# A feature-major U by VectorE block transposes in a conditioned residual kernel, with a new order of work at the head

## Chip, cores and metric

The kernel runs on one NeuronCore of a Trainium2 chip. The metric is the device time of one execution in microseconds, taken as the median of several runs. The profile is of one execution of the same program and has its own time.

## The reference, cut to what matters

Two layers are applied to x (2 batches, 2048 rows, 512 features, float32), each added to its input.

```python
U = (mu @ W_dec + b_dec).reshape(B, 513, 30)      # mu: 2 x 256, W_dec: 256 x 15390
weight = U[:, :-1] @ V ; bias = U[:, -1] @ V       # V: 30 x 512
x1 = x + (x @ weight + bias)
...
h = ln(ln(x1, pw_g[path], pw_b[path]), cp_g[c], cp_b[c])
t = ln(x1, tm_g[c], tm_b[c]) ; s = ln(x1, ms_g[k], ms_b[k])
m, n, r = x1 + mlp_ln(memory), x1 + mlp_ln(noise), x1 + mlp_ln(resource)
cat = [w0*h, w1*t, w2*m, w3*n, w4*r, w5*s]         # w = softmax(aw), 3072 features
out = x1 + ln(silu(cat @ int_W1 + b1) @ int_W2 + b2) * g + be
```

The matrix x @ weight is never built. The kernel computes (x @ U) @ V with the rank-30 factor U, so U must lie with the 512 input features on partitions, in 4 chunks of 128, before TensorE can multiply x by it.

## The kernel before, in words

The 4096 rows are worked in 32 tiles of 128 rows, which alternate between the batches. Each engine has one program, ordered by hand, and semaphores tie them together. Names used below:

- `decode(j)`, 16 steps: TensorE multiplies the conditioning vector (cond, 32 columns, 2 of them real) by a piece of W_dec (960 KB) which SyncE has loaded into one of 8 ring slots. Two steps, one per half of the 256 rows, fill one of 8 banks with 32 partitions x 480 columns in each of 4 partition quadrants. `dec_used` counts the steps.
- `evacuate(m)` on ScalarE copies bank m to `Ur`. There U is a row vector on partitions c*32+b (chunk c, batch b). `to_features` moves it by 16 small DMAs (12 issued by GpSimd, 4 by ScalarE) into `Uf`, with features on partitions. VectorE adds b_dec to `Uf` and writes it four times into `Ust` as high and low parts (`ust_ready`).
- `prefill(p)`: the product of a tile's x with the X block of int_W1 for tiles 2 to 13, done between the decode steps so that TensorE has work while W_dec arrives. `pre_high(p)` (ScalarE) and `pre_low(p)` (VectorE) split the operand into two parts, and `pre_keep(p)` (ScalarE) saves the result in the stash. A product is 12 matmuls: high x high, high x low, low x high in 4 chunks.
- `embed(t)`: x @ Ust of a tile; `embedded` (ScalarE) and `stacked` (VectorE) make the operand of `expand(t)`, which multiplies by V. `first_sum` adds x, `x_stats` and GpSimd's `rstd` make the norm, `x_norm` (ScalarE) writes xhat.
- `scaled`, `scale_rows` and `h_first`/`h_gain` make the operands t, s and h. TensorE transposes them (`transpose_t/s/h`), ScalarE and VectorE split them (`t_high`/`t_split` and so on), and `t_product`, `s_product`, `h_product` follow. `silu`, `transpose_z`, `z_split`, `second_product`, `out_stats`, `out_scaled`, `out_row` finish a tile.
- The blocks of int_W1 (`BLK_T`, `BLK_S`, `BLK_H`) and int_W2 (`BLK_W2`), and the small MLPs' weights (`MLP1`, `MLP2[0..2]`) come through the ring after W_dec. `block_high` (ScalarE) and `t_low`, `s_low`, `h_low` (VectorE) split them.
- `mlp_second(m)` and `sum_parts` finish the conditioning vectors, `low_rank_product` and `offset_product` make the small operands VWst and BT.
- All loads but the gathers (`gathers`, GpSimd) are issued by SyncE in one order: the head's order is written out at L437 to L482 and L455 on is the part behind the decode.
- From tile 2 on each engine repeats `step(n)`. Tiles 2 to 13 are the kept ones, whose X product was made ahead by `prefill`.

## Time and profile before

| | |
|---|---|
| median of 3 runs | 614.84 us (613.6 to 614.91) |
| the profiled execution | 613.73 us, span 611.9 us |
| TensorE busy | 584.0 us, 95% |
| VectorE, ScalarE, GpSimd busy | 416.7, 204.7, 389.4 us |
| bytes moved | 102.07 MB |

The span runs from the first to the last instruction; what lies around it in the profiled execution is 1.8 us. A group of instructions is given by its line in the kernel, its engine and the tiles that it writes and reads. The idle time printed with an instruction is what its engine waited just before it.

### The profile page before, as it was taken

The numbers are of one execution on the slowest core, as the hardware profiler recorded it, in microseconds if no ns is written. First come the engines' busy times: TensorE is split into PE (matmuls) and PEld (weight loads), VectorE is DVE, ScalarE is ACT, GpSimd is POOL, SyncE is SP. The second block draws the span as 40 slices with busy tenths as digits, with TensorE's granted clock in tenths as the row PEclk, the third lists the DMA queues.
The fourth block names the chain that finished last, engine by engine and source line by source line (L and its number), as shares of the span: only waits on it lengthen the run. The fifth ranks groups of instructions, "written<-read, shape, count | busy, mean of one in ns | idle before, by whom it ended". The sixth has DMA issues, their size and how long they took to land.

```text
span 611.9 us, 9087 instructions
## 1 busy us (share of the span) xinstructions
PE 584.0 (95%) x2924; PEld 453.9 (74%) x2924; DVE 416.7 (68%) x750; ACT 204.7 (33%) x346; POOL 389.4 (64%) x499
## 2 busy tenths in 40 slices
PE   0999889999999999999999999999999999999995
PEld 0455446588888888888888888888888888888784
DVE  4311277688888888888766676676666666667754
ACT  4333454333334333334233223233322332232222
POOL 1011467568888888888676676666677766666720
PEclk9999999999999999999999999999999999999999
DMA  8999996425544555555433334435443333443201
GB/s 333 406 403 364 351 353 231 148 69 159 160 143 142 162 165 164 147 181 159 144 93 125 125 119 143 123 126 142 142 141 113 130 116 123 120 142 116 79 19 51
DMA packets 51039, 102.07 MB, mean 167 GB/s; under 512 B 9646, under 2 KB 22190, under 8 KB 50876
## 3 DMA queue, kind: packets, MB, share of 16 engines
q1 hardware_dynamic: 38496, 59.54, 28.3%
q0 software_dynamic: 12160, 42.04, 22.4%
q8 instruction: 18, 0.29, 0.2%
q14 instruction: 17, 0.14, 0.1%
q10 hardware_dynamic: 348, 0.06, 0.1%
HBM read 93.11 MB, written 8.39 MB: 166 GB/s over the span
## 4 chain that ended last, share of the span: by engine, by line
PE 83%; DMA 8%; DVE 3%; SPq 2%; issue 2%; POOL 2%; ACT 1%; DVEq 0%; POOLq 0%
PE bank L744 22%; PE bank L745 22%; PE bank L746 22%; PE bank L738 8%; DMA ring<-in_W_dec 5%; DMA ring<-in_int_W 3%; PE bank L795 2%; SPq L333 2%; PE bank L732 2%; PE bank L814 1%; PE bank L810 1%; PE bank L805 1%; DMA pwt<-in_pw,idx 1%; DVE bn L1250 1%; PE bank L886 0%
## 5 line engine op out<-in xcount | busy, mean ns | idle before, releaser
L744 PE MATMUL bank<-W,ops 128*128 128x512 f32 x432 | 177.8, 412 | 0.0
L745 PE MATMUL bank<-W,ops 128*128 128x512 f32 x432 | 171.1, 396 | 0.0
L746 PE MATMUL bank<-W,ops 128*128 128x512 f32 x432 | 170.8, 395 | 0.0
L592 ACT ACTIVATE ops<-bank 128x512 fp32r<-128x512 f32 x97 | 57.1, 590 | 154.0 <-PE bank L738 154.0
L744 PEld LDWEIGHTS bank<-W,ops 128*128 128x128 f32 x432 | 81.7, 189 | 25.2 <-issue 8.4
L746 PEld LDWEIGHTS bank<-W,ops 128*128 128x128 f32 x432 | 81.4, 188 | 19.5
L745 PEld LDWEIGHTS bank<-W,ops 128*128 128x128 f32 x432 | 81.7, 189 | 14.7
L1245 DVE TENSOR_TENSOR ops<-bank,ops 128x512 fp32r<-128x512 f32 x97 | 66.2, 683 | 12.5 <-ACT ops L592 12.5
L1250 DVE BATCH_NORM_STATS2 bn<-h 128x6 f32<-128x512 f32 x32 | 22.2, 693 | 55.2 <-POOL h L1082 55.2
L1022 POOL TENSOR_SCALAR ve<-mv 128x1 f32<-128x1 f32 x94 | 31.3, 333 | 38.7 <-DVE mv L1254 35.3
L641 ACT ACTIVATE xhat<-x,nm,rs 128x512 f32<-128x512 f32 x32 | 26.1, 816 | 82.0 <-POOL nm L1035 82.0
L744 PE MATMUL bank<-W,zop 128*128 128x512 f32 x124 | 49.6, 400 | 0.4 <-DVE zop L1245 0.4
L1082 POOL TENSOR_TENSOR h<-h,pwt 128x512 f32<-128x512 f32 x32 | 47.6, 1489 | 2.5
L745 PE MATMUL bank<-W,zop 128*128 128x512 f32 x124 | 49.0, 395 | 0.0
L746 PE MATMUL bank<-W,zop 128*128 128x512 f32 x124 | 49.0, 395 | 0.0
L1071 POOL TENSOR_TENSOR xop<-stash,xop 128x512 fp32r<-128x512 f32 x18 | 23.2, 1290 | 39.6 <-ACT xop L563 39.6
L1371 DVE SCALAR_TENSOR_TENSOR o<-o,mv,gbc 128x512 f32<-128x512 f32 x31 | 47.7, 1540 | 0.0
L1047 POOL DMA_INDIRECT ctt<-in_ct,idx x32 | 40.4, 1261 | 8.7 <-issue 5.2
L1080 POOL TENSOR_TENSOR h<-xhat,pwt 128x512 f32<-128x512 f32 x32 | 42.8, 1336 | 2.9 <-ACT xhat L641 1.9
L648 ACT ACTIVATE ht<-h,nm,rs 128x512 f32<-128x512 f32 x32 | 26.1, 816 | 54.1 <-POOL nm L1035 54.1
L333 POOL DMA_DIRECT2D Uf<-Ur x12 | 6.5, 565 | 56.6 <-ACT Ur L549 56.6
L1091 POOL TENSOR_TENSOR xb<-x,bebc 128x512 f32<-128x512 f32 x32 | 42.0, 1314 | 0.6
(145 smaller groups left out, 1080.7 us busy)
## 6 DMA issues: line engine op xcount, KB each, us to landing
ring<-in_W_dec SPq DMA_DIRECT2D x16, 960.0 KB, 12.1
x<-in_x SPq DMA_DIRECT2D x32, 256.0 KB
out<-xb SPq DMA_DIRECT2D x31, 256.0 KB
stash<-in_xT SPq DMA_DIRECT2D x30, 256.0 KB, 5.2
ring<-in_int_W SPq DMA_DIRECT2D x4, 1024.0 KB, 9.2
xraw<-in_xT SPq DMA_DIRECT2D x14, 256.0 KB, 2.8
mnr_row<-in_mnr SPq DMA_DIRECT2D x3, 768.0 KB, 7.6
idxrep<-in_rows SPq DMA_DIRECT2D x32, 64.0 KB, 3.8
```

What stands on the lines that cost most here:

```text
L592: nc.scalar.activation(dst.rearrange("p c t -> p (c t)"), bank[:, :], ACT.Copy).then_inc(done, 1)
L738: last = nc.tensor.transpose(dst[:, c * P:(c + 1) * P], src[:, c * P:(c + 1) * P], ident)
L744: nc.tensor.matmul(bank[:, :], op[:, HI, c, :], w[:, HI, c, :], start=start and c == 0, stop=False)
L745: nc.tensor.matmul(bank[:, :], op[:, HI, c, :], w[:, LO, c, :], start=False, stop=False)
L746: last = nc.tensor.matmul(bank[:, :], op[:, LO, c, :], w[:, HI, c, :], start=False, stop=stop and c == KC - 1)
L1022: nc.gpsimd.tensor_scalar(ve[:, which:which + 1], mv[:, which, 1:2], EPS, 1.0, ALU.add, ALU.mult) \
L1047: pool.indirect_dma_start(out=dst[:, s, :], out_offset=None, in_=d[table], in_offset=bass.IndirectOffsetOnAxis(ap=idx[:, s, col:col + 1], ...
L1080: nc.gpsimd.tensor_tensor(h1[:, :], xhat[:, :], pwt[:, s, 0:D], ALU.mult).then_inc(h1_part, 1)
L1082: nc.gpsimd.tensor_tensor(h1[:, :], h1[:, :], pwt[:, s, D:2 * D], ALU.add).then_inc(h1_ready, 1)
L1091: nc.gpsimd.tensor_tensor(xb[:, f.row, :], x1[:, f.slot, :], bebc[:, :], ALU.add).then_inc(xb_ready, 1)
L1245: nc.vector.tensor_tensor(dst.rearrange("p c t -> p (c t)"), bank[:, :], hi.bitcast(F32).rearrange("p c t -> p (c t)"), ALU.subtract).then ...
L1371: nc.vector.scalar_tensor_tensor(out=o[:, :], in0=o[:, :], scalar=mv[:, 2, 0:1], in1=gbc[:, :], op0=ALU.subtract, op1=ALU.mult).then_inc(u ...
```

## The change

U takes another way to the feature partitions. The host orders W_dec so that bank m = 2c+h holds, for chunk c and half h of the ranks, in quadrant g the columns (rank, feature) of 15 ranks x 32 features. One VectorE transpose of each bank in 32x32 blocks (`turn`) puts the feature on the partition. The addition of b_dec then reads `UT` with a stride of 32 elements. `evacuate`, `to_features` and their DMAs are gone. A piece of W_dec is now one run of 7680 bytes per partition, where it had been four of 1920.

The constants are loaded in two parts: what the offsets and selections need (`BL` and what lies behind it, 347.5 of 601.5 KB) comes late (`picks_in`), behind MLP2. The order of loads, and of each engine's head, is new, and so is part of each `step`.

```diff
+            def turn(m):
+                v.wait_ge(dec_used, 2 * (m + 1))
+                nc.vector.transpose(UT[:, m * BANK:(m + 1) * BANK], u_bank_of(m)[:, 0:BANK]).then_inc(u_row, 1)
+            for j in range(2 * DECS):
+                if j % 2 == 1:
+                    turn(j // 2)
+                if j in PRE_AFTER and PRE_AFTER.index(j) + 2 < NPRE - 2:
+                    pre_low(PRE_AFTER.index(j) + 2)
...
-            pre_low(NPRE - 1)
-            v.wait_ge(u_in_pool, 16 * 3 * KC)
-            v.wait_ge(u_in_act, 16 * KC)
+            v.wait_ge(u_row, DECS)
             for b in range(B):
-                last = nc.vector.tensor_tensor(Uf[:, b, :, :], Uf[:, b, :, :], bdec[:, :, :], ALU.add)
+                last = nc.vector.tensor_tensor(
+                    Uf[:, b, :, :], UT.rearrange("p (c r j) -> p j c r", c=KC, j=Q)[:, b, :, :], bdec[:, :, :], ALU.add)
...
+            pre_low(NPRE - 2)
+            pre_low(NPRE - 1)
```

Loads (SyncE):

```diff
-                    load(sp, cst_in, (cst[:, :], d["cst"]))
+                    load(sp, cst_in, (cst[:, 0:AT_BL], d["cst"][:, 0:AT_BL]))
...
             load_ring(sp, MLP1)
+            load_pre(NPRE - 2)
+            load_x(Tile(1))
             load_rows(Tile(0))
-            load_pre(NPRE - 2)
-            load_pre(NPRE - 1)
+            load_rows(Tile(1))
             load_ring(sp, BLK_T)
+            load_pre(NPRE - 1)
             load_ring(sp, MLP2[0])
-            load_x(Tile(1))
             load_ring(sp, MLP2[1])
             load_ring(sp, MLP2[2])
+            load(sp, picks_in, (cst[:, AT_BL:CST], d["cst"][:, AT_BL:CST]))
             load_ring(sp, BLK_S)
-            load_rows(Tile(1))
             load_ring(sp, BLK_H)
-            load_rows(Tile(2))
+            load_x(Tile(2))
             load_ring(sp, BLK_W2)
-            load_x(Tile(2))
+            load_rows(Tile(2))
```

Heads of ScalarE (first part) and TensorE (second part), as lines taken out and put in:

```diff
             embedded(t0)
+            x_high(t1)
             block_high(T_, WT, BLK_T, t_block_hi)
-            x_high(t1)
             x_norm(t0)
+            embedded(t1)
             t_high(t0)
-            embedded(t1)
+            evict_part((mlp_used, 4), mlp_part)
+            block_high(S_, WS, BLK_S, s_block_hi)
             pre_keep(NPRE - 1)
-            block_high(S_, WS, BLK_S, s_block_hi)
-            evict_part((mlp_used, 4), mlp_part)
+            x_high(t2)
+            h_norm(t0)
             s_high(t0)
...
+            embed(t0)
+            prefill(NPRE - 1, FRONT)
             pe.wait_ge(silu_ready, 1)
             transpose_rows(HIDT, hid, hidT_sum)
-            embed(t0)
-            prefill(NPRE - 1, FRONT)
+            expand(t0)
+            x_half(t0, 0)
             prefill(NPRE - 1, BACK)
-            expand(t0)
             mlp_second(0)
             embed(t1)
             mlp_second(1)
-            x_half(t0, 0)
+            mlp_second(2)
             transpose_t(t0)
-            mlp_second(2)
+            transpose_s(t0)
             x_half(t0, 1)
             sum_parts(sel_m, mlp_part, mlp_sum, start=False)
-            transpose_s(t0)
+            expand(t1)
             x_half(t1, 0)
-            expand(t1)
```

In GpSimd's head `x_low(t0)` comes before `gathers(t0)`, `x_low(t1)` behind `rstd(0, t0)`, and `gathers(t1)` behind `rstd(1, t0)`. In VectorE's head both `one_hot` come first and `scale_rows` ahead of `scaled` for tile 0. Behind the offset product TensorE does `s_product(t1)` before `transpose_h(t1)` and `sum_parts(sel_bt, ...)`.

In every step: TensorE does `transpose_h(m)` behind `t_product(m)`, where it came before; ScalarE does `h_high(m)` before `z_high(c)`; VectorE does `scaled` before `scale_rows`, `h_split` before `out_scaled`, and `one_hot` ahead of `s_split`.

## Rows read from the trace of the kernel before

**Rows 1.** The page's busy time: engine, us, share of span, instructions

```profile
PE 584.0 (95%) x2924; PEld 453.9 (74%) x2924; DVE 416.7 (68%) x750; ACT 204.7 (33%) x346; POOL 389.4 (64%) x499
```

**Rows 2.** Waits of TensorE over the span: total us, times, longest

```profile
PE bank L732 <- DMA ring<-in_W_dec: 17.2, 3, 15.6
PE bank L874 <- ACT part L596: 1.7, 2, 0.9
PE bank L795 <- DVE Ust L1240: 1.2, 1, 1.2
PE bank L795 <- POOL xop L1071: 0.8, 1, 0.8
...
PE bank L738 <- DVE tt L1289: 0.2, 1, 0.2
```

**Rows 3.** Windows: length, PE, PEld, DVE, ACT, POOL busy; clock, DMA share, GB/s

```profile
2.00:15.40 13.40, 0.00 (x0) 0.00 (x0) 7.59 (x14) 6.21 (x10) 0.51 (x3) 1.00 0.99 379
...
61.50:77.00 15.50, 14.25 (x59) 7.65 (x60) 4.05 (x14) 6.37 (x9) 6.59 (x8) 1.00 1.01 358
...
200.00:300.00 100.00, 100.00 (x504) 82.66 (x504) 87.60 (x158) 37.80 (x65) 85.14 (x107) 1.00 0.52 158
```

**Rows 4.** Timeline of SyncE's loads: start, us of the issue

```profile
2.12 0.66 SPq L333 DMA_DIRECT2D cst<-in_cst  x1
...
64.93 4.33 SPq L333 DMA_DIRECT2D ring<-in_res_W  x1
```

**Rows 5.** DMA issues: count, KB each, median us from issue to landing

```profile
ring<-in_res_W SPq DMA_DIRECT2D x1, 1024.0 KB, 18.4
...
cst<-in_cst SPq DMA_DIRECT2D x1, 601.5 KB, 9.0
...
Uf<-Ur POOLq DMA_DIRECT2D x12, 7.5 KB, 4.9
```

**Rows 6.** The chain that ended last, 59 to 90 us: start, us, what

```profile
47.88 13.64 DMA ring<-in_W_dec
...
69.30 16.73 DMA ring<-in_int_W
...
86.06 2.01 ACT W L584
```

**Rows 7.** Timeline of ScalarE in the head

```profile
62.65 0.57 ACT L549 ACTIVATE Ur<-bank 128x480 f32<-128x480 f32 x1 [1.19 <-PE bank L732]
...
68.55 1.28 ACT L588 ACT_TABLE_LOAD   x1
...
85.02 0.60 ACT L545 ACTIVATE stash<-bank 128x512 f32<-128x512 f32 x1
```

**Rows 8.** Timeline of VectorE in the head

```profile
67.56 0.69 DVE L1188 TENSOR_TENSOR ops<-stash,ops 128x512 fp32r<-128x512 f32 x1 [11.49 <-ACT ops L541]
...
72.78 0.48 DVE L1235 TENSOR_TENSOR Uf<-Uf,cst 128x120 f32<-128x120 f32 x2 [3.53 <-DMA Uf<-Ur]
73.30 0.67 DVE L1238 CAST Ust<-Uf 128x240 fp32r<-128x240 f32 x3
74.00 0.41 DVE L1240 TENSOR_TENSOR Ust<-Uf,Ust 128x240 fp32r<-128x240 f32 x1
...
120.23 0.75 DVE L1347 SCALAR_TENSOR_TENSOR BT<-BT,cst,bank 128x512 fp32r<-128x512 f32 x1 [0.70 <-ACT BT L600]
```

**Rows 9.** Timeline of TensorE in the head

```profile
89.97 0.48 PE L744 MATMUL bank<-W,xop 128*128 128x512 f32 x1
```

**Rows 10.** Timeline of one kept step, VectorE and TensorE, and VectorE's end

```profile
249.42 0.68 DVE L1245 TENSOR_TENSOR zop<-bank,zop 128x512 fp32r<-128x512 f32 x1
250.03 1.65 DVE L1371 SCALAR_TENSOR_TENSOR o<-o,mv,gbc 128x512 f32<-128x512 f32 x1
...
250.47 0.40 PE L744 MATMUL bank<-W,zop 128*128 128x512 f32 x1
...
604.29 0.75 DVE L1371 SCALAR_TENSOR_TENSOR o<-o,mv,gbc 128x512 f32<-128x512 f32 x1
```

More of the change, by code:

```diff
@@ L375, in u_bank_of @@
             return pU[m % len(pU)]
-        def to_features(eng, got, half, rows):
-            eng.wait_ge(u_row, DECS // 2 * (half + 1))
-            at, n = half * P // 2, P // 2
-            load(eng, got, *[(Uf[at:at + n, b, c, :],
-                              Ur[c * Q + b:c * Q + b + 1, at * RANK:(at + n) * RANK].rearrange(
-                                  "o (p r) -> o p r", r=RANK)) for c, b in rows])
-        U_ROWS = [(c, b) for c in range(KC) for b in range(B)]
         block = ctx.enter_context(nc.Block())
@@ L941, in _ @@
             offset_product()
+            s_product(t1)
             transpose_h(t1)
@@ L945, in _ @@
             low_rank(t0)
-            s_product(t1)
+            embed(t2.plus(1))
+            low_rank(t1)
             pe.wait_ge(bt_ready, 1)
             offsets(t0)
-            low_rank(t1)
             offsets(t1)
@@ L952, in _ @@
             transpose_z(t0)
-            embed(t2.plus(1))
             h_product(t1)
@@ L1382, in _ @@
             t0, t1, t2 = Tile(0), Tile(1), Tile(2)
+            one_hot(t0)
+            one_hot(t1)
             stacked(t0)
```

116 lines of the change are left out of this document (51 added, 65 removed).

## Prediction, made before the changed kernel was run

> **What bounds the kernel now.** I read the page's busy times first, then TensorE's waits, then windows, and last the chain through the head. TensorE is busy for 584.0 of the 611.9 us [rows 1]. In the middle, from 200 to 300 us, it is busy for all of 100.00 us at the full granted clock, while VectorE has 87.60 and GpSimd 85.14 [rows 3]. No reordering can make that part shorter, since no matmul is added or removed; it can only open gaps. What is to be gained lies ahead of tile 2's step. TensorE's whole list of waits [rows 2] holds 15.6 us until the first piece of W_dec is there, 1.6 us more on later pieces (17.2 in three waits; the last of them is about 0.5, when piece 15 lands at 47.88 + 13.64 = 61.52 [rows 6], and the other is about 1.2), 1.2 for Ust, 0.8 for the low part of tile 1's x, 0.2 for t, and 1.7 in two waits for a partial sum that ScalarE copies. Behind the start these are about 5.5 us.
>
> The head is bound by transfers too. The windows show a DMA share of 0.99 and 379 GB/s until 15.4 us, and 1.01 and 358 GB/s from 61.5 to 77.0 [rows 3]. The chain says the same: it goes from the load of BLK_S (69.30 + 16.73 = 86.03) to ScalarE's high part of it (86.06, 2.01 us) [rows 6]. So a wait that disappears on TensorE is kept as a gain only if the next block has also landed.
>
> **The start.** The constants (601.5 KB, issued at 2.12, landed 9.0 us later [rows 4, 5]) stand in the queue ahead of decode piece 0. Of them 347.5 KB are taken out, which is 356 thousand bytes, at 379 GB/s [rows 3] 0.9 us. TensorE's first wait, all of it for that queue, becomes shorter by this: -0.9 us. Pieces of 7680 bytes in place of 1920 move the same bytes; the trace has no such run of W_dec, so I bound the stream by 5% either way. Between the second piece and piece 15 TensorE waits for nothing, so a faster stream is worth only the last 0.5 us, which I count: piece 15 comes 0.9 earlier by the start, and the 8 small Uf transfers that ran beside the stream are gone. Running total -1.4 at the end of the decode. A stream that is 5% slower would give 46 x 0.05 = 2.3 us back (46 us from the first landing to 61.52); this is the upper bound of this term.
>
> The Trainium skill, page "DMA: Bandwidth & Descriptors", section "Why small descriptors are slow (HBM only)", gives each packet a fixed cost of about 3 cycles beside one per 32 bytes. By it 1920 bytes cost 63 cycles and 7680 cost 243 in place of 252, so the stream would be 3.6% shorter, an estimate of 1.7 us over 46. The sum would stay as it is, since TensorE is what paces the stream's middle; no row here compares the two sizes of W_dec.
>
> **The way of U.** Removed are 8 copies by ScalarE (0.57 each [rows 7]) and 16 small transfers; added are 8 VectorE transposes of the same 128x480 banks. Not shown before; from below I take the copy's 0.57, from above 1.3, more than twice that, and use 0.6. They lie where VectorE is idle: it had waited 11.49 us for work when it began at 67.56 [rows 8]. Only the last transpose is on a path: piece 15 is decoded by 61.3, then 0.6, the addition 0.48 (0.96 if the stride doubles it), the three casts 0.67 and the low part 0.41 [rows 8], with links some 2.5 us: Ust is ready by 64, against 74.4 before. The embedding of tile 0 comes near 71.4 (TensorE was ready for it 1.2 us before 74.4; 1.4 earlier now, and the four small transposes of the hidden rows, 0.4, come behind it), so all bounds of these prices are hidden by 7 us. The 1.2 us wait for Ust [rows 2] goes. If the transposes did cost 1.3 the answer is the same.
>
> **What takes its place.** With the embedding at 71.4, the stash load for prefill 11 is next. It now stands behind the loads for tile 1 and BLK_T. About 3.5 MB of queue and some 0.7 MB of gathers after 60.2 at 358 GB/s [rows 3] put it at 71 to 72; ScalarE waits for it, and behind it in ScalarE's program stand the table load (1.28 us [rows 7]), the SiLU of the MLPs, a `pre_keep` and `embedded(t0)`. The last is then near 73.8, the stack near 74.7, and `expand(t0)`, which TensorE reaches at 73.5, waits 1.2 us. So the Ust wait is replaced by one of equal size (bounds 0 to 2.5).
>
> MLP2's last block landed at 64.93 + 18.4 = 83.3 [rows 4, 5]. Now there are tile 1's x and rows ahead of it, 0.33 MB net, but all is 1.4 earlier: 82.7 or so. TensorE is there near 81.2 (from 74.7: 0.3 for `expand`, twice 1.4 for half products, then some 0.9 for each of two MLP2 parts and the addition of b2, and 0.6 for an embedding; my estimates, as such a group takes about this beside the rows shown) and waits 1.5. The waits of 0.8, 0.2 and the first 0.8 of the partial sum (1.8 together [rows 2]) are gone in exchange.
>
> **The point that decides.** Both these waits are absorbed by a later one. BLK_S landed at 86.03. It starts from a queue 1.4 us earlier, less 0.4 for the small packets of U that are gone, but has 0.69 MB more ahead of it (tile 1's rows 0.33, the deferred constants 0.36), at 358 to 379 GB/s 1.9 us. That gives 86.1. ScalarE needs 2.01 us for its high part [rows 6], and `pre_keep(11)`, which was done at 85.02 before that block [rows 7], now comes behind it: 0.6 more. HID[1] is free only then, so tile 1's `x_half`, which stood at 89.97 [rows 9], can begin at 88.8 at the earliest: -1.1 us, whatever TensorE saved before. From here `t_product`, `s_product`, `h_product` of tile 0 follow as before; VectorE has the low parts of S and H and both splits done about 0.5 us before TensorE asks, by the same row prices (0.69 a split, 1.3 a half block). I carry -1.1.
>
> Behind `offset_product`, `s_product(t1)` and `transpose_h(t1)` now come ahead of the sum, so ScalarE's copy is hidden and the second partial-sum wait (0.9, [rows 2]) goes. `offsets(t0)` comes sooner behind the sum than before, when a product of 2.8 us stood between; ScalarE's high part and VectorE's 0.75 [rows 8] must now fit under `low_rank`, `embed(t3)` and `low_rank`, which leaves 0.3 open. Net -0.6.
>
> **The steps.** In a kept step VectorE's `z_split` starts at 249.42 and takes 0.68, and `second_product` starts at 250.47 [rows 10]: 0.37 us of slack. `z_high` moves behind `h_high`, 0.6 later, but VectorE did not wait for it. Putting `h_split` ahead of `out_scaled` changes nothing there. I cost the steps and the tail at nothing.
>
> Sum: -1.1 - 0.6 = -1.7 us of span, 611.9 to 610.2, and with 1.8 around it 612.0 for the profiled execution. That one (613.73) stood 1.1 under the median of 614.84, so the median becomes 613.1 (-0.3%).
>
> **Rivals.** (A) The block path does not bind: BLK_S lands earlier because the wide pieces run faster and leave room. Then all the waits behind the start go (5.5 less the 1.2 between the first pieces is 4.3, and 0.9 from the start): -5.2, 609.6. For it speaks that every new order was put where a wait stood; against it, the DMA share of 1.01. Chance 0.17 for -3 or more.
>
> (B) The deferred constants and tile 1's rows come too early in the queue and BLK_S is late by another 1.3 us, as with 330 GB/s in place of 358 for the 6 MB ahead of it. The gain of 1.1 is gone, and only the 0.6 or less is left: 614.3, no change that can be measured. Chance 0.22.
>
> (C) Slower: `out_scaled` moves to a place where GpSimd is adding in `h_first`. It took 1.65 us beside GpSimd's work and 0.75 alone at the end [rows 10], so up to 0.9 us can pass to `h_first`, then to `h_stats`, `first_sum`, xhat and `z_split`. 0.2 of it is caught by `one_hot`, and 0.37 is slack: 0.33 us in each of 12 kept steps is 4.0 us, so -1.7 + 4.0 gives 617.1. It decides from 0.51 us of lateness per step on (slack plus 1.7/12). Against it: the same two work on one another today. Chance 0.1. The Trainium skill, page "SBUF — State Buffer", names the port pair that VectorE and GpSimd share, exclusively and for a whole instruction, and would have the loser blocked fully. By that rule the 0.9 passes on whole and rival C's 617.1 holds; the 1.65 against 0.75 agrees that they collide.
>
> (D) The transposes or the strided addition are late enough to delay `embed(t0)`: they would have to cost 7 us more. Chance 0.02; it gives nothing, 614.8.
>
> **Numbers.** The forecast itself has 0.49, with its own range 611.8 to 614.4 (the expand wait and the block's landing within 1.3 us). The whole range runs from 610.4, which leaves out the far end of A, to 615.8, which leaves out C. What a measurement here can tell is 0.2%, 1.2 us, so faster means under 613.6. Most of the forecast's 0.49 (0.43), A's 0.17 and a little of B make 0.62; within is 0.26 (B and the forecast's rest, D); slower is 0.12 (C and a slow W_dec stream).
>
> **What would show it.** TensorE's first matmul near 14.7 in place of 15.6; no wait for Ust; transposes of 0.6 us in VectorE's idle stretch; a wait of TensorE at `expand(t0)`, one at MLP2's last block, and the longest at tile 1's `x_half` behind ScalarE's `pre_keep`; no gaps between 200 and 300 us. The prediction is wrong if W_dec's landings run slower than 2.5 us a piece, if BLK_S lands off 86.1 by more than 1 us, or if a wait on `z_split` recurs in the steps.

## The result, and the profile after

The changed kernel takes 617.81 us (median of 6 runs, 617.36 to 619.36) where the one before takes 614.88 (6 runs, 613.6 to 615.28): a ratio of 1.0059 (95% interval 1.0047 to 1.0070). It is slower by 2.9 us, and I had forecast 1.7 faster. The profiled execution took 617.85 us with a span of 616.0, against 611.9. These two executions are 4.1 us apart and the medians 2.9, since the profiled one of before (613.73) was one of its fastest; marks read from single executions carry such scatter.

The busy times after, against [rows 1]. TensorE's number of instructions is the same; ScalarE and VectorE have less to do, and nothing of that is in the time.

```profile
PE 586.7 (95%) x2924; PEld 455.5 (74%) x2924; DVE 405.1 (66%) x758; ACT 199.8 (32%) x338; POOL 384.4 (62%) x487
```

TensorE's waits after (total us, times, longest), against [rows 2]:

```profile
PE bank L713 <- DMA ring<-in_W_dec: 15.5, 2, 14.4
PE bank L776 <- POOL xop L1054: 1.3, 1, 1.3
PE bank L725 <- ACT stash L534: 1.3, 1, 1.3
PE bank L725 <- DVE ops L1169: 1.0, 1, 1.0
PE bank L725 <- DVE zop L1235: 0.8, 3, 0.4
PE bank L719 <- DVE zop L1235: 0.8, 1, 0.8
PE bank L848 <- DMA ring<-in_res_W: 0.8, 1, 0.8
PE bank L786 <- DVE stack L1258: 0.7, 1, 0.7
PE bank L795 <- DVE BT L1339: 0.6, 1, 0.6
```

The waits for Ust, tile 1's x and both partial sums are gone. In their place stand one for prefill 11's operand (L1169), the stack, MLP2's last block, ScalarE's `pre_keep` (L534), and then four that are not in my sum: tile 2's x (L776), BT (L795), and `zop` twice (0.78 at L719, 0.20 at L725). Before had a wait for `zop` too, the one of 0.4 near the end that stands in both kernels; the prediction's "whole list" leaves it out.

Windows, against [rows 3] (the last one again in the middle of the W_dec stream), and the stretch from 91 to 141 us of after and of before:

```profile
2.00:15.40 13.40, 0.98 (x8) 0.23 (x8) 8.54 (x15) 6.85 (x11) 0.52 (x3) 1.00 0.99 386
61.50:77.00 15.50, 13.78 (x55) 7.71 (x52) 5.55 (x18) 6.06 (x9) 3.07 (x3) 1.00 1.02 366
200.00:300.00 100.00, 99.90 (x506) 82.09 (x504) 84.38 (x157) 37.00 (x63) 84.56 (x107) 1.00 0.51 155
30.00:45.00 15.00, 15.00 (x81) 9.20 (x79) 4.47 (x7) 3.64 (x7) 0.00 (x0) 1.00 1.02 413
...
91.00:141.00 50.00, 46.98 (x253) 31.20 (x252) 32.59 (x57) 19.54 (x29) 33.89 (x36) 1.00 0.48 140
```

```profile
91.00:141.00 50.00, 49.08 (x269) 33.57 (x268) 37.29 (x63) 18.95 (x28) 33.82 (x41) 1.00 0.47 154
```

TensorE is idle for 3.0 us between 91 and 141 us, where it had been idle for 0.9. U's way looks as forecast. VectorE after, against [rows 8]:

```profile
61.69 0.68 DVE L1189 STREAM_TRANSPOSE UT<-bank 128x480 f32<-128x480 f32 x1 [0.93 <-PE bank L713]
62.41 0.66 DVE L1222 TENSOR_TENSOR Uf<-UT,cst 128x120 f32<-128x120 f32 x2
63.10 0.68 DVE L1226 CAST Ust<-Uf 128x240 fp32r<-128x240 f32 x3
63.81 0.41 DVE L1228 TENSOR_TENSOR Ust<-Uf,Ust 128x240 fp32r<-128x240 f32 x1
```

A transpose takes 0.68, the strided addition 0.66 for both batches, and Ust is ready at 64.2 in place of 74.4. ScalarE at the point that I called decisive, against [rows 6, 7]:

```profile
87.38 2.00 ACT L565 ACTIVATE W<-ring,wsm 128x2048 fp32r<-128x2048 f32 x1 [0.71 <-DMA ring<-in_int_W]
89.29 0.58 ACT L534 ACTIVATE stash<-bank 128x512 f32<-128x512 f32 x1
91.14 0.63 ACT L547 ACTIVATE xop<-xraw 128x512 fp32r<-128x512 f32 x1 [1.28 <-DMA xraw<-in_xT]
```

What TensorE waits for further on, in the changed kernel. GpSimd makes the low part of tile 2's x (`xop`) only behind `h_first(t1)`, and ScalarE's high part of z (`zop`) stands behind `h_norm(t2)`, which waits for GpSimd:

```profile
105.55 1.60 POOL L1065 TENSOR_TENSOR h<-h,pwt 128x512 f32<-128x512 f32 x1
107.11 1.27 POOL L1054 TENSOR_TENSOR xop<-xraw,xop 128x512 fp32r<-128x512 f32 x1
```

```profile
127.50 0.81 ACT L629 ACTIVATE ht<-h,nm,rs 128x512 f32<-128x512 f32 x1 [1.51 <-POOL nm L1018]
128.22 0.58 ACT L573 ACTIVATE zop<-bank 128x512 fp32r<-128x512 f32 x1
```

These marks on TensorE place the loss. A "mark" is the start of that group in the timeline (us):

| mark | before | after | difference |
|---|---|---|---|
| first matmul | 15.57 | 14.42 | -1.15 |
| tile 1's x product | 89.97 | 90.01 | 0.0 |
| low-rank product | 102.53 | 102.30 | -0.2 |
| embedding of tile 2 | 107.06 | 108.43 | +1.4 |
| offsets of tile 0 | 122.43 | 124.19 | +1.8 |
| second product of tile 0 | 127.68 | 130.06 | +2.4 |
| embedding of tile 4 | 141.54 | 144.29 | +2.75 |
| end of the span | 611.93 | 616.05 | +4.1 |

So there are three parts: a head's first part that should have gained 1.1 and shows 0.2, a second part (102 to 141 us) that loses 3.0, and the steps, which lose 1.4 more, all between two single executions.

### The profile page after: what moved, and what is told of

The parts are those of the page before. It is cut to its first block, busy times and chain, and to the rows that moved or that the text cites. A ratio compares the mean times of both kernels' runs of the same rounds, so it can differ in the third digit from the quotient of the medians.

```text
span 616.0 us, 9076 instructions
## 1 busy us (share of the span) xinstructions
PE 586.7 (95%) x2924; PEld 455.5 (74%) x2924; DVE 405.1 (66%) x758; ACT 199.8 (32%) x338; POOL 384.4 (62%) x487
## 3 DMA queue, kind: packets, MB, share of 16 engines
q0 software_dynamic: 11776, 41.95, 22.4%
## 4 chain that ended last, share of the span: by engine, by line
PE 59%; POOL 14%; DMA 11%; DVE 7%; issue 6%; ACT 2%; SPq 1%; POOLq 0%; DVEq 0%; ACTq 0%
PE bank L725 16%; PE bank L726 16%; PE bank L727 16%; DMA pwt<-in_pw,idx 7%; PE bank L719 5%; POOL h L1065 3%; POOL h L1063 3%; POOL ctt L1030 2%; DMA ring<-in_W_dec 2%; DVE bn L1240 2%; PE bank L713 2%; POOL rs L1013 2%; POOL ve L1005 2%; PE bank L776 1%; DMA stash<-in_xT 1%
## 5 line engine op out<-in xcount | busy, mean ns | idle before, releaser
L725 PE MATMUL bank<-W,ops 128*128 128x512 f32 x432 | 176.5, 409 | 1.1 <-DVE ops L1169 1.0
L725 PEld LDWEIGHTS bank<-W,ops 128*128 128x128 f32 x432 | 81.8, 189 | 29.9 <-issue 10.1
L1235 DVE TENSOR_TENSOR ops<-bank,ops 128x512 fp32r<-128x512 f32 x97 | 66.1, 682 | 8.8 <-ACT ops L573 8.6
L1240 DVE BATCH_NORM_STATS2 bn<-h 128x6 f32<-128x512 f32 x32 | 22.2, 693 | 74.4 <-POOL h L1065 74.4
L1005 POOL TENSOR_SCALAR ve<-mv 128x1 f32<-128x1 f32 x94 | 33.2, 354 | 48.2 <-DVE mv L1244 44.8
L1054 POOL TENSOR_TENSOR xop<-xraw,xop 128x512 fp32r<-128x512 f32 x14 | 18.0, 1286 | 57.1 <-ACT xop L547 57.1
L1030 POOL DMA_INDIRECT ctt<-in_ct,idx x32 | 43.3, 1352 | 14.0 <-DMA idx<-in_idx 6.2
L725 PE MATMUL bank<-W,zop 128*128 128x512 f32 x124 | 49.8, 402 | 0.8 <-DVE zop L1235 0.8
L1065 POOL TENSOR_TENSOR h<-h,pwt 128x512 f32<-128x512 f32 x32 | 46.2, 1444 | 2.5
L1030 POOL DMA_INDIRECT sgt<-in_ms_g,idx x32 | 33.3, 1040 | 12.1 <-issue 12.1
```

Of the source, the lines that this page charges most:

```text
L725: nc.tensor.matmul(bank[:, :], op[:, HI, c, :], w[:, HI, c, :], start=start and c == 0, stop=False)
L1005: nc.gpsimd.tensor_scalar(ve[:, which:which + 1], mv[:, which, 1:2], EPS, 1.0, ALU.add, ALU.mult) \
L1030: pool.indirect_dma_start(out=dst[:, s, :], out_offset=None, in_=d[table], in_offset=bass.IndirectOffsetOnAxis(ap=idx[:, s, col:col + 1], ...
L1054: nc.gpsimd.tensor_tensor(xop[:, s, LO, :, :], x_rows(a), xop[:, s, HI, :, :].bitcast(F32), ALU.subtract).then_inc(x_lo, 1)
L1065: nc.gpsimd.tensor_tensor(h1[:, :], h1[:, :], pwt[:, s, D:2 * D], ALU.add).then_inc(h1_ready, 1)
L1235: nc.vector.tensor_tensor(dst.rearrange("p c t -> p (c t)"), bank[:, :], hi.bitcast(F32).rearrange("p c t -> p (c t)"), ALU.subtract).then ...
```

## Experiments

Each kernel was compared with runs of the kernel before on the same chip (medians between 614.5 and 614.9). The order below is by question, not by time.

| run | median us | ratio, 95% interval |
|---|---|---|
| e1, before with U's way alone | 613.64 | 0.9993 [0.9983, 1.0002] |
| e2, before with the new steps | 615.16 | 1.0008 [0.9999, 1.0017] |
| e5, before with the constants split | 613.37 | 0.9984 [0.9975, 0.9992] |
| e3, after with the old steps | 618.07 | 1.0057 [1.0045, 1.0070] |
| e4, after, x_low(t2) first | 617.29 | 1.0040 [1.0026, 1.0055] |
| e6, after, GpSimd's old head | 621.45 | 1.0118 [1.0103, 1.0133] |
| e7, after, TensorE's old order at BT | 618.60 | 1.0064 [1.0044, 1.0085] |
| e9, before, U, split, new loads | 619.04 | 1.0072 [1.0060, 1.0084] |
| e10, after, loads in the pause | 628.21 | 1.0214 [1.0198, 1.0230] |
| e13, after, tile 2's rows earlier | 621.39 | 1.0099 [1.0082, 1.0117] |
| e14, after, gathers(t1) earlier | 620.69 | 1.0092 [1.0077, 1.0108] |
| e15, both of these | 625.21 | 1.0171 [1.0157, 1.0185] |
| e16, e15, x_low(t2) and z_high first | 624.60 | 1.0163 [1.0149, 1.0177] |
| e17, after, three engines' places | 618.73 | 1.0067 [1.0054, 1.0080] |
| e18, after, old second part on four engines | 614.83 | 1.0004 [0.9995, 1.0013] |
| e8, best: U, split, loads in the pause | 611.22 | 0.9950 [0.9937, 0.9963] |
| e11, e8 without U's way | 612.66 | 0.9966 [0.9953, 0.9978] |
| e12, e8 with GpSimd's new head | 621.60 | 1.0100 [1.0082, 1.0118] |

**The parts alone: e1, e2, e5.** e1 has the whole first diff of the change and W_dec's new layout, with every order of before. e2 has only the steps:

```diff
-                z_high(c)
                 if m.exists():
                     h_high(m)
+                z_high(c)
...
-                    transpose_h(m)
                 if kept(m):
                     t_product(m, FRONT)
                 if m.exists():
                     t_product(m, BACK if kept(m) else range(KC))
+                    transpose_h(m)
...
```

e5 has only the split (the second part behind the last piece of W_dec):

```diff
-                    load(sp, cst_in, (cst[:, :], d["cst"]))
+                    load(sp, cst_in, (cst[:, 0:AT_BL], d["cst"][:, 0:AT_BL]))
...
+            load(sp, picks_in, (cst[:, AT_BL:CST], d["cst"][:, AT_BL:CST]))
             sp.wait_ge(dec_used, slot[MLP1] + SLOTS + 1)
```

> The kernel before with the way of U alone changed: W_dec's layout, VectorE's transposes of the banks, the strided addition, no ScalarE copies and no relayout transfers. Every load, every head order and every step stays as in the kernel before, except that the low parts of tiles 10 and 11 of the prefill come behind Ust. Theory 1 (the new way of U is sound, the loss comes from the orders around it): the 1.18 us wait for Ust goes, and the second waits stay, so the time is 0.3 to 1.2 us under before, 613.7 to 614.6. Theory 2 (the new way of U itself costs, by the transposes on VectorE or by the wide pieces): it is slower than before by 1 us or more.

> The kernel before with the new orders inside every step alone: the transposes of h behind the t product, the high part of h before that of z, scaled before scale_rows, h_split before out_scaled, one_hot ahead of s_split. The head and the way of U are those of before. Theory 1 (the step orders lose some tenths of a us in some of the steps, as the marks of the steps drift apart by 1.4 us between tile 4 and tile 31): 1.0 to 1.8 us slower than before, 615.9 to 616.7. Theory 2 (the drift is an after-effect of the late head and of loads that come later): no change, within 0.4 us of before.

> The kernel before with the constants alone loaded in two parts: 254 KB ahead of decode piece 3 of the queue's head as before, 347.5 KB behind decode piece 15, where the transfer engines had a pause. The way of U, the heads and the steps are those of before. Theory 1 (an earlier start is mostly lost to TensorE's clock: in the kernel before the matmuls' pitch went from 0.43 to 0.23 us at 23.7 us, in the changed one at 24.3, though it began 1.15 us earlier): the first matmul is near 14.5, the third decode step only 0.2 to 0.4 earlier than before, and the time 0 to 0.4 us under before. Theory 2 (the start counts in full, as the prediction had it): the third decode step and the end come 0.9 to 1.1 us earlier.

U's way alone is worth less than can be told: the Ust wait of 1.2 is gone, but TensorE then waits 1.56 for tile 1's x in place of 0.78, and 1.60 for the partial sum behind S's high part in place of 0.82: 0.8 us more at each of two later waits. The steps alone cost nothing that can be told. The split gains 0.16%; the first matmul is at 14.60, and 1.0 us is still there at tile 1's x product (88.95), so the start counted in full there.

**Taking back one engine: e3, e4, e6, e7.** e3 is the changed kernel with e2's places taken back, e6 with GpSimd's head as before, and e7 with TensorE's order behind the offset product as before. e4 moves one line of GpSimd:

```diff
-                h_first(t1)
                 x_low(t2)
+                h_first(t1)
```

> The changed kernel with the step orders of before. Theory 1 (step orders): 1.0 to 1.8 us under the changed kernel, 616.0 to 616.8, and the marks of its steps stay a constant distance from those of before. Theory 2 (after-effect of the head): the drift stays, the time stays within 0.4 of 617.8.

> The changed kernel with one GpSimd call put back: the low part of tile 2's x comes before h_first of tile 1 again, as before. Theory 1 (the 1.35 us wait of TensorE at tile 2's embedding is lost for good): 1.0 to 1.4 us under the changed kernel, 616.4 to 616.8. Theory 2 (a later wait takes it over, that for BT or for h_first's result, since h of tile 1 comes 1.3 us later): within 0.4 of 617.8, with the wait for BT or for the z parts longer by as much.

> The changed kernel with the whole head order of GpSimd as in the kernel before: the low part of tile 1's x ahead of rstd of tile 0, the gathers of tile 1 ahead of rstd(1) of tile 0, the low part of tile 2's x ahead of h_first of tile 1, rstd(1) of tile 1 ahead of both residual sums. Theory 1 (GpSimd's head order is what lost the time behind tile 1's X product): no wait of TensorE at tile 2's embedding, GpSimd's rstd(1) of tile 1 near 110 and not 113.3, and 1.5 us or more under the changed kernel, 616.3 or less. Theory 2 (the order of TensorE behind the offset product is what counts, as moving one call in the fourth kernel brought only some 0.5 us): 617.3 and not less.

> The changed kernel with TensorE's order behind the offset product as in the kernel before: the sum for BT ahead of the s product of tile 1, the embedding of tile 3 behind the transposes of z. Theory 1 (that order lost what lies between 1.36 us at tile 2's embedding and 2.75 at tile 4's: the waits for BT 0.61 and for parts of z 0.78 and 0.20): the waits of 0.61 and 0.78 go, that of 0.9 for the partial sum comes back or is hidden, and the time is 0.5 to 1.4 us under the changed kernel, 616.4 to 617.3. Theory 2 (those waits come from h of tile 1, which GpSimd makes late, whatever TensorE's order): no change, within 0.3 of 617.8.

None takes the loss away. e3 says that it is not the steps' order: with the old one its loss at tile 4 is 2.6 us, and behind it 1.7 where the changed kernel has 1.4. e6 opens a wait of 1.9 at the stack; in e7 the waits for BT (0.61) and `zop` (0.78) are gone as hoped, and one of 2.0 opens at `transpose_h(t1)`, which now comes ahead of `s_product(t1)` while VectorE's `h_gain(t1)` keeps its late place. In e4 the embedding of tile 2 is as early as before (107.23), yet the offsets of tile 0 are at 124.43. e4's 617.29 is not clear of the changed kernel's 617.81 either: the intervals overlap. The two timelines of e4, GpSimd's (one line) and VectorE's, say why so little came of it:

```profile
106.29 1.61 POOL L1065 TENSOR_TENSOR h<-h,pwt 128x512 f32<-128x512 f32 x1
```

```profile
107.93 0.69 DVE L1240 BATCH_NORM_STATS2 bn<-h 128x6 f32<-128x512 f32 x1 [1.17 <-POOL h L1065]
108.73 0.18 DVE L1244 BATCH_NORM_AGGREGATE mv<-bn 128x2 f32<-128x6 f32 x1
108.83 1.26 DVE L1235 TENSOR_TENSOR ops<-bank,ops 128x512 fp32r<-128x512 f32 x2
```

VectorE's new order has `h_stats(t1)` ahead of the splits of t and s (L1235), so whoever holds back GpSimd's h holds back both, and TensorE waited 0.74 at `t_product(t1)`. The order of one engine can be judged only with those of the others.

**TensorE's granted clock is a part of these times.** I read the granted clock in windows of 1 us from 15 to 165 us for every profiled execution. It is 1.00 throughout in the changed kernel, the one before, e1 to e6, e8, e11 and e18. In the other nine it drops to 0.50, the lower of its two levels, for some microseconds, each time behind or in a wait of TensorE; these waits are 1.7 to 11.2 us long, and e6 waits 1.9 us without a drop. In e17 and in e12 (us, PE, PEld, DVE, ACT, POOL busy; clock, DMA share, GB/s):

```profile
91.00:126.00 35.00, 31.56 (x181) 19.00 (x181) 25.05 (x37) 13.78 (x19) 26.06 (x26) 1.00 0.50 165
126.00:129.00 3.00, 3.00 (x10) 2.52 (x11) 0.69 (x1) 1.78 (x3) 2.13 (x4) 0.50 0.00 0
```

```profile
112.00:118.00 6.00, 5.61 (x13) 4.00 (x14) 2.58 (x7) 1.19 (x3) 3.79 (x6) 0.50 0.50 162
```

Added up, what is missing to 1.00 is 1.7 us in e13 and e17, 3.4 in e7, e9, e14, e15 and e16, 5.1 in e12 and 6.8 in e10. My estimate is that the times of these runs hold up to that much beside their waits: all of it in e17, where TensorE is busy throughout, and less where the drop lies in the wait itself, as from 78 to 85 us in e10 and at first in e14, e15 and e16. e7 shows it in its own executions: three with a mean granted clock of 0.996 to 0.999 take 616.9 to 617.6 us, three with 0.993 take 619.6 to 620.8. So its median of 618.60 does not say that its order is slower than the changed kernel's. Two of the changed kernel's six executions have 0.994 and take 618.6 and 619.4; the other four take 617.4 to 617.9, and the profiled one (617.85) shows no drop, so its loss against before is there without one.

**The loads: e9, e10, e13 to e16.** e9 is e1 with the split and the changed kernel's order of loads; e10 is the changed kernel with tile 1's x, the operand of prefill 11 and the late constants issued before MLP1, in a pause of the queue from 59 to 61 us:

```diff
+            load_pre(NPRE - 2)
+            load_x(Tile(1))
+            load(sp, picks_in, (cst[:, AT_BL:CST], d["cst"][:, AT_BL:CST]))
             sp.wait_ge(dec_used, slot[MLP1] + SLOTS + 1)
             load_ring(sp, MLP1)
-            load_pre(NPRE - 2)
-            load_x(Tile(1))
             load_rows(Tile(0))
-            load_rows(Tile(1))
...
             load_ring(sp, BLK_S)
+            load_rows(Tile(1))
```

e13 and e14 (e15 has both):

```diff
             load_ring(sp, BLK_H)
-            load_x(Tile(2))
+            load_rows(Tile(2))
...
             h_first(t0)
+            gathers(t1)
             rstd(1, t0, mv2_ready, r2_ready)
```

> The kernel before with U's new way, the constants in two parts and the changed kernel's order of SyncE's loads; every engine's order of work stays that of before. Theory (the changed kernel loses in the engines' orders behind tile 1's x, not in its loads): tile 1's x is there early, so no wait of 1.5 us on it near 79 us; BLK_S lands near 87.4 as in the changed kernel, ScalarE's high part of it ends near 89.4, and TensorE waits about 1.5 us for the partial sum that ScalarE copies behind it. Tile 1's x product near 89.5, tile 2's embedding near 106.5, time 613.0 to 614.0. Rival (the loads of the changed kernel cost it its time, BLK_S, BLK_H and W2 one after the other): tile 2's embedding at 108 or later and a time of 616.5 or more.

> The changed kernel with its loads alone changed: the stash row set for prefill 11, tile 1's x and the late constants are issued in the pause of the stream behind piece 15 (59 to 61 us), where the queue had nothing to do, and tile 1's rows go behind BLK_S. All engines' orders are the changed kernel's. Theory (engines' orders): BLK_S lands about 1.3 us earlier, tile 1's x product begins near 88.3, but GpSimd's queue still holds the low part of tile 2's x, and tile 2's embedding comes at 107.5 to 108.4; time 616.3 to 617.3 against 617.8 of the changed kernel. Rival (loads): the whole loss of the head goes, tile 2's embedding near 105.5 and a time of 612 to 614.

> The changed kernel with tile 2's indices loaded behind BLK_H and its x behind BLK_W2, as before; all else the changed kernel's. Theory (the index load, last in the queue, holds the gathers of tile 2): GpSimd's gathers of tile 2 end near 99.8 in place of 101.4, tile 2's embedding near 107, time 616.4 to 617.0. Rival (the gathers of tile 1 start too late, and the indices are there by then anyway): gathers of tile 2 end at 101 or later, time 617.4 to 618.2.

> The changed kernel with GpSimd's gathers of tile 1 ahead of rstd(1, t0), in the 3.6 us in which GpSimd waits for tile 0's second mean; all else the changed kernel's. Theory (late gathers of tile 1 hold back those of tile 2): gathers of tile 1 end near 88.3, those of tile 2 near 98, embedding of tile 2 near 105, time 615 to 616.5. Rival (tile 2's indices land late): the gathers of tile 2 wait for the indices until about 98 and end at 101 or later; embedding and time as in the changed kernel, 617.4 to 618.2.

> Both edits together. If the two hold in series (either alone hides the other), only this one recovers: gathers of tile 2 end near 98, embedding of tile 2 near 105.5, tile 4's near 141.5, time 614.6 to 615.8. If neither is the cause: 617.4 to 618.2, with the embedding at 108 again.

> e15 with GpSimd's low part of tile 2's x ahead of h_first(t1), and ScalarE's z_high(t0) right behind silu(t0), ahead of s_high(t2) and h_norm(t2). Theory (the wait of 0.8 at tile 0's second product comes from z_high behind h_norm, which itself waits for GpSimd): that wait goes, tile 0's second product 0.6 to 0.8 earlier than in e15 beside what the embedding gains, time 613.4 to 614.8. Rival (the waits behind tile 2's embedding are set by TensorE's order at BT): second product as late as in e15, time within 0.3 of e15.

Every theory stated here fell on the time. Of the rivals, e9's had the right sign ("616.5 or more"): with the engine orders of before, the new order of loads does cost 4.5 us, up to 3.4 of them the low clock behind its waits. It is not the cause in the changed kernel, since e18 below keeps these loads. The waits say more than the times, which hold the low clock too. e9: with before's ScalarE, which asks for prefill 11's operand ahead of the SiLU, the later load costs 2.5 us at the hidden rows, and tile 2's indices, last in the queue, hold GpSimd:

```profile
100.92 1.03 POOL L1030 DMA_INDIRECT ctt<-in_ct,idx  x1 [6.36 <-DMA idx<-in_idx]
```

e10: the new VectorE head asks for `one_hot(t1)` before tile 0's stack, and I had moved its rows behind BLK_S:

```profile
84.03 0.29 DVE L1202 TENSOR_SCALAR OH<-idxrep,cst 128x128 fp32r<-128x128 int32 x1 [13.55 <-DMA idxrep<-in_rows]
```

TensorE then waited 11.2 us at the stack: this edit broke a dependence of my own making and says nothing on the loads. e13 (first line) and e15 (second): ScalarE's new order has `x_high(t2)` ahead of `h_norm(t0)`, so a later x holds h of tile 0, which TensorE and the gathers of tile 2 need. ScalarE waited 1.28 us in the changed kernel, 5.39 and 9.18 here:

```profile
95.29 0.63 ACT L547 ACTIVATE xop<-xraw 128x512 fp32r<-128x512 f32 x1 [5.39 <-DMA xraw<-in_xT]
```

```profile
99.00 0.63 ACT L547 ACTIVATE xop<-xraw 128x512 fp32r<-128x512 f32 x1 [9.18 <-DMA xraw<-in_xT]
```

In e14 the earlier gathers had the same effect: tile 2's x was used at 93.41 in place of 91.14 (3.83 us of waiting for its load), and the gathers of tile 2 waited 6.86 us for their indices. In e16 the second product of tile 0 is 2.3 us earlier than in e15 (135.99 for 138.25), as `z_high` no longer waits, but the time is only 0.6 less: tile 4's embedding is 1.1 earlier.

**The second part of the head as a whole: e17 and e18.** "The change" shows the new order of this part for TensorE only; e17's and e18's edits, read backwards, show it for the others. e17 puts back the four places that hang together on GpSimd, VectorE and ScalarE, and leaves TensorE's order:

```diff
 GpSimd
-                h_first(t1)
                 x_low(t2)
+                h_first(t1)
+                rstd(1, t1, mv2_ready, r2_ready)
                 residual(t0)
                 residual(t1)
-                rstd(1, t1, mv2_ready, r2_ready)
 VectorE
-            h_stats(t1)
             t_split(t1)
-            s_split(t1)
             stacked(t2)
+            h_stats(t1)
+            s_split(t1)
+            h_gain(t1)
             first_sum(t2)
...
-            h_gain(t1)
 ScalarE
             silu(t0)
+            z_high(t0)
             s_high(t2)
             h_norm(t2)
-            z_high(t0)
```

e18 has the order of before from tile 1's norm to the first step on all four engines. On VectorE it also puts the two halves of W2's low part behind `split_bt`, on TensorE the sum for BT ahead of `s_product(t1)`. Loads, U's way, the head's first part and the steps stay the changed kernel's. Parts of the edit on VectorE and TensorE:

```diff
 VectorE
-            w2_low(0)
-            scaled(t2)
             split_vw()
-            h_gain(t1)
-            w2_low(1)
             scale_rows(t2)
             h_split(t1)
             split_bt()
+            w2_low(0)
+            w2_low(1)
+            z_split(t0)
+            scaled(t2)
...
 TensorE
-            s_product(t1)
             transpose_h(t1)
             pe.wait_ge(vwst_ready, 1)
             sum_parts(sel_bt, bt_part, bt_sum)
             low_rank(t0)
-            embed(t2.plus(1))
-            low_rank(t1)
+            s_product(t1)
             pe.wait_ge(bt_ready, 1)
             offsets(t0)
+            low_rank(t1)
...
```

> The changed kernel with four places put back together: GpSimd does x_low(t2) before h_first(t1) and rstd(1, t1) before the residuals; VectorE does t_split(t1) and stacked(t2) before h_stats(t1), and h_gain(t1) before first_sum(t2); ScalarE does z_high(t0) right behind silu(t0). TensorE's order stays the changed kernel's. Theory (these four hang together and make the loss behind tile 2's embedding): tile 2's embedding at 107.2, the offset product at 111.8, offsets of tile 0 at 122.8, second product at 128.0 without its wait of 0.8, tile 4's embedding at 141.7, against 144.3; time 615.0 to 615.9. Rival (the loss is in TensorE's new order at BT or spread over the steps): second product later than 129.5 and time 617 or more.

> The changed kernel with the whole order of before from tile 1's norm to the first step on all four engines; loads, U's way, the first part of the head and the steps are the changed kernel's. Theory (the second part of the head makes the loss): tile 4's embedding at 141.3 to 141.8, time 614.8 to 615.9, level with before within 0.2%. Rival (the loss comes from the first part, the loads or the steps): tile 4's embedding later than 143, time 617 or more.

e18 takes 614.83 us against 614.67, a ratio of 1.0004: level with before. So the order of this part is the cause of the measured slowdown; e3 says that the steps' order is not. In e17 the embedding of tile 2 came at 106.34 and the offset product at 110.86, 2.1 earlier than in the changed kernel (0.9 of it from ahead of the low-rank product). Then TensorE waited 3.2 us for BT (L1339; 0.6 in the changed kernel), and behind that wait came the low clock shown above, 1.7 us: both together cost more than was gained. The theory's time fell, and the rival's two signs (second product later than 129.5, it came at 131.09; 617 or more) were met, though by BT's place on VectorE and the clock. VectorE and GpSimd in e17:

```profile
119.02 2.56 DVE L1345 TENSOR_TENSOR W<-ring,W 128x1024 fp32r<-128x1024 f32 x1
121.50 1.74 DVE L1287 TENSOR_TENSOR st<-xhat,sgt 128x512 f32<-128x512 f32 x1
123.27 0.69 DVE L1235 TENSOR_TENSOR ops<-bank,ops 128x512 fp32r<-128x512 f32 x1
123.88 0.74 DVE L1339 SCALAR_TENSOR_TENSOR BT<-BT,cst,bank 128x512 fp32r<-128x512 f32 x1
```

```profile
119.20 1.28 POOL L1063 TENSOR_TENSOR h<-xhat,pwt 128x512 f32<-128x512 f32 x1
120.56 2.13 POOL L1065 TENSOR_TENSOR h<-h,pwt 128x512 f32<-128x512 f32 x1
```

VectorE's same two operations in the changed kernel, where GpSimd was not in `h_first` at that time, and BT in e18, ahead of W2:

```profile
120.20 1.22 DVE L1345 TENSOR_TENSOR W<-ring,W 128x1024 fp32r<-128x1024 f32 x1
121.33 0.68 DVE L1287 TENSOR_TENSOR st<-xhat,sgt 128x512 f32<-128x512 f32 x1
```

```profile
119.21 0.75 DVE L1339 SCALAR_TENSOR_TENSOR BT<-BT,cst,bank 128x512 fp32r<-128x512 f32 x1 [0.77 <-ACT BT L581]
119.88 4.08 DVE L1345 TENSOR_TENSOR W<-ring,W 128x1024 fp32r<-128x1024 f32 x2
```

With both `w2_low` and `scale_rows(t2)` ahead of `split_bt`, BT comes at 123.4 in the changed kernel, 123.6 in e4 and 123.9 in e17, whether tile 2's embedding is late (108.43) or not (107.23 and 106.34). So in e17 TensorE waited longer there. e4's gain was gone before that, at `t_product(t1)` (0.74) and at the stack (0.21).

**The version that beats both: e8, and what U is worth in it: e11, e12.** e8 is e5 with U's way, three loads in the pause behind piece 15, and two changes on ScalarE:

```diff
+            load_pre(NPRE - 2)
+            load_x(Tile(1))
+            load(sp, picks_in, (cst[:, AT_BL:CST], d["cst"][:, AT_BL:CST]))
             sp.wait_ge(dec_used, slot[MLP1] + SLOTS + 1)
             load_ring(sp, MLP1)
             load_rows(Tile(0))
-            load_pre(NPRE - 2)
             load_pre(NPRE - 1)
...
             pre_keep(NPRE - 1)
-            block_high(S_, WS, BLK_S, s_block_hi)
             evict_part((mlp_used, 4), mlp_part)
+            block_high(S_, WS, BLK_S, s_block_hi)
...
-            x_norm(t2)
             x_high(t2.plus(1))
+            x_norm(t2)
```

> The kernel before with the new way of U, the constants in two parts, the stash of tile 12, tile 1's x and the second part of the constants issued right behind decode piece 15, ahead of the wait for a free ring slot, the copy of the partial sum ahead of the high part of BLK_S, and the high part of tile 3's x ahead of the norm of tile 2. All other orders are those of before. Theory 1 (the waits of TensorE in the head can be taken away one by one where their cause is a late load or a busy ScalarE): the waits of 1.56 for tile 1's x and of 1.60 for the partial sum, which stand in the first kernel, go, and the time is 1.5 to 3 us under before, 611.7 to 613.2. Theory 2 (the head is bound by the transfers of the weight blocks): the waits move to the MLP2 blocks and BLK_S, and it stays within 0.7 us of the first kernel's 613.6.

> The fastest version so far (611.2) without U's new way: ScalarE's copies and the 16 small transfers are back, loads and engines' orders stay. If U's new way is worth its wait of 1.2 us at tile 0's embedding once the loads behind it are early, this takes 612.2 to 612.8. If it is worth nothing, because BLK_S's landing absorbs it, 611.0 to 611.6.

> The fastest version so far (611.2) with GpSimd's head in the changed kernel's order (rstd before x_low, gathers of tile 1 behind rstd, h_first of tile 1 before the low part of tile 2's x, residuals before the last rstd), all else unchanged. Theory (this order puts the low part of tile 2's x behind h_first of tile 1 and the gathers): TensorE waits 1 to 2 us at tile 2's embedding or x product or for rstd of tile 1, tile 4's embedding comes 1.4 to 2.5 us later than 138.0, time 612.6 to 613.8. Rival (GpSimd's order alone is harmless, only together with the others'): 611.0 to 611.7.

e8 takes 611.22 us, ratio 0.9950. Tile 1's x product is at 86.23 (89.97 before), tile 4's embedding at 138.00 (141.54). All of its waits of 0.2 us and more but those for W_dec:

```profile
PE bank L776 <- POOL xop L1054: 0.8, 1, 0.8
PE bank L725 <- DVE zop L1235: 0.6, 2, 0.4
PE bank L725 <- DVE W L1207: 0.4, 1, 0.4
PE bank L856 <- ACT part L577: 0.3, 1, 0.3
PE bank L719 <- DVE tt L1279: 0.2, 1, 0.2
```

They add up to 2.3 us; in the kernel before they were 4.3 (3.9 in the lines of [rows 2] and 0.4 for `zop`). Without U's way the same kernel takes 612.66. By the medians U's way is worth 1.4 us here, by the two ratios 1.0; the two sets of executions do not overlap (610.87 to 611.78 against 612.58 to 613.70), while the intervals of the ratios just do. In e1, with the loads of before, the waits for tile 1's x and the partial sum grew instead. GpSimd's new head alone (e12) costs this kernel 10 us, where I had forecast at most 2.6: `x_low(t1)`, now behind `rstd(0, t0)`, made TensorE wait 3.9, tile 1's t 3.0 and tile 2's x 1.3, and some 5 us of the low clock lie around these waits.

## Why the prediction was wrong, by its steps

- **The start, -0.9: right.** The first matmul came 1.15 us earlier, in e5 0.97. In the changed kernel's profiled execution only 0.3 of it was left at the third decode step (25.06 in place of 25.36); in e5 1.1 was (24.25).
- **W_dec's pieces: right within the bounds.** 413 GB/s from 30 to 45 us, against 404 before. The estimate from the Trainium skill, "DMA: Bandwidth & Descriptors", "Why small descriptors are slow (HBM only)", was 3.6%; these windows show 2.2%. From 20 to 60 us the changed kernel moved 383 GB/s and before 396, at DMA shares of 0.94 and 1.04, so the stream as a whole did not become shorter. The wait of 0.5 for piece 15 is gone.
- **U's way and its price: right.** 0.68 in place of 0.6 for a transpose, 0.66 for the strided addition, Ust at 64.2.
- **What takes its place: right in kind.** I named 1.2 us at `expand(t0)` and 1.5 at MLP2's last block; 1.0 at prefill 11, 0.7 at the stack and 0.8 at that block were measured.
- **The point that decides, -1.1: right in mechanism, hidden in the profiled execution.** TensorE did wait 1.3 us for `pre_keep(11)` behind S's high part. S landed at 87.4 where I had 86.1, which is past the 1 us that I had named as a sign of being wrong. The changed kernel, e3, e4, e7, e17 and e18 have the same program up to there. In their six executions S's high part starts at 86.4 to 87.4, and tile 0's first product at 91.9 to 92.9 in place of 93.06: a gain of 0.2 to 1.15 us, 0.9 in the middle, with the changed kernel's own profile at the low end and e18 (91.92) near the other. So the size is about right, and the profile of the changed kernel shows little of it by the luck of one execution. Between it and e18 0.7 us was there by 25 us (below).
- **"Net -0.6" for all that lies behind tile 0's products: the step that failed.** Tile 0's products did "follow as before" (9.44 us from the first of them to the low-rank product, 9.47 before). Behind them, from the low-rank product to tile 4's embedding, where the sum has -0.6, it took 42.0 us in place of 39.0: +3.0. I traced TensorE and ScalarE through this part and neither GpSimd's nor VectorE's queue. The wait for the second partial sum (0.9) went as forecast. Against it came 1.35 us for tile 2's x behind `h_first(t1)`, 0.61 for BT where I had left "0.3 open", 0.78 for `zop` because `z_high(t0)` stands behind `h_norm(t2)`, which waits for GpSimd's rstd, and 0.2 for the next one. These are 2.9 us of waits less 0.9; some 1.0 of the 3.0 us in that stretch is in no wait that the profile names. In e18, with the old order of this part, the stretch takes 39.5.
- **The price of BT's cover was a single row.** I asked whether ScalarE's high part and VectorE's 0.75 fit under three TensorE groups, and did not count what else stands ahead of them on VectorE: `w2_low(1)` (1.2), which the change puts there, and then `scale_rows(t2)` (0.7) and `h_split(t1)` (0.7), which already stood ahead of BT before.
- **The steps "at nothing": the order is right (e2, e3), the size is not.** From tile 4's embedding to the end it is 470.4 us before and in e5, 470.8 in e1, 471.1 in e8, 471.2 in e2 and e18, 471.8 in the changed kernel, 472.1 in e3. These are single executions. The differences stand at a few steps, 0.1 to 0.7 us each: one of 0.65 is in e2 and e3 (14.77 us for a step of 14.1), and one of 0.35 at the step that begins near 323 us in every kernel with both U's way and the split (17.27 us in place of 16.92). I have no experiment that settles them. They turn e18's gain of 0.7 us at tile 4 into +0.2 at the end.
- **Rival C (slower) had the right sign, but the wrong place, and its 617.1 is near the 617.8 by luck.** It put the collision of VectorE with GpSimd into the steps. e2 and e3 exclude that as the main loss. The collision itself is there in e17's head: 2.56 against 1.22, and 1.74 against 0.68 us, beside `h_first(t2)`. In the changed kernel these two operations ran clear of it, so it is not what delayed BT there; but its `scale_rows(t1)` ran beside `h_first(t1)` and took 1.76 us in place of 0.92. The Trainium skill, "SBUF — State Buffer", section "Who interferes with whom", gives the shared pair to whoever issues first, for the whole instruction, and blocks the other fully. The rows agree only in part: VectorE's 2.56 began 0.18 us ahead of GpSimd's first operation, which took its usual 1.28; behind it both were slower, 1.74 on VectorE and 2.13 on GpSimd, which took 1.27 in the changed kernel.
- **Rivals A and B** did not happen: the waits did not all go, and BLK_S's landing did not cost the gain.

What stays open: which one place of the second part costs how much. e4, e7 and e17 each put a piece back and got -0.5, +0.8 and +0.9 us. The first is within the scatter, and the other two hold the low clock. Only e18, all four engines, is level. The shown cause is the part as a whole. BT's place on VectorE behind `w2_low` is what e17 ran into, but no run moves `w2_low` alone, and in e7, with TensorE's order of before at BT, there was no wait for it; so the split between VectorE's and TensorE's order is not shown.

## What to carry to other kernels

A new order of one engine must be traced through every other engine's queue up to the next point where they meet: list for each moved operation what now stands ahead of it on its own engine, with durations, not only what it depends on. A gain at a wait is kept only up to the next bound: U's way gave nothing measurable alone and 1.0 to 1.4 us once the loads behind it were early. When waits are added up against a time, read TensorE's granted clock in windows behind each wait too: in e17 the clock took 1.7 us beside the 3.2 of the wait. And when undoing one engine's part makes a kernel slower still, undo a stretch of time on all engines, not one engine over all time.

## What the runs showed that I had not expected

- A 128x480 float32 transpose in 32x32 blocks from a bank takes 0.68 us on VectorE, as much as a 128x512 addition (0.69).
- The matmuls of 512 columns at the start come every 0.43 us and later every 0.23. The windows' granted clock reads 1.00 on both sides. In e17's stretch at a granted 0.50 such matmuls also come every 0.43 us, so I read the start as TensorE's lower level too (512 columns in 0.43 us are 1.2 GHz, the other level being 2.4), though the granted clock does not show it there. The first matmul was at 15.6, 14.6, 14.4 and 14.4 us in before, e5, e18 and the changed kernel, and the faster pace began near 23.7, 22.4, 23.0 and 24.5, though the program up to there is the same in the last two. Each matmul at the lower level costs 0.2 us more, so these two executions differ by 0.7 us from there on (25.06 against 24.35 at the third decode step). The medians have this in them as scatter.
- A wait of TensorE can cost more than its length. In e17 the granted clock fell behind a wait of 3.2 us, and that took an estimated 1.7 us more (above).

The changed kernel, and e18, around that point:

```profile
24.50 0.40 PE L726 MATMUL bank<-W,ops 128*128 128x512 f32 x1
24.74 0.40 PE L727 MATMUL bank<-W,ops 128*128 128x512 f32 x1
25.06 0.61 PE L713 MATMUL bank<-ring,cst 128*32 128x480 f32 x4
```

```profile
22.74 0.51 PE L725 MATMUL bank<-W,ops 128*128 128x512 f32 x1
23.09 0.39 PE L726 MATMUL bank<-W,ops 128*128 128x512 f32 x1
```
